# Rotary embedding of the queries: the sine product moved to VectorE and the exchange of halves moved to transfers

## The reference

```python
x = x + layernorm(attention(layernorm(x)))
x = x + layernorm(ffn(layernorm(x)))

# attention, per sequence
q = (x @ Wq.T).reshape(n, H, D);  kv = x @ Wkv.T;  kv_head = x @ Wkvh.T
kv_head = cumsum(kv_head * exp(cumsum(log_sigmoid(x @ Wg.T), shifted by one token)))
k = rope(outer(kp, kh));  v = outer(vp, vh)      # one key/value vector, one factor per head
o = softmax(causal(rope(q) @ k.T / sqrt(D))) @ v
return o @ Wout.T

# rope on a vector t with halves t1, t2
concat([t1 * cos - t2 * sin, t2 * cos + t1 * sin])
```

## Time and profile before

| | us |
|---|---|
| median of three runs | 1042.84 |
| lowest and highest run | 1042.63, 1044.16 |
| span of the profiled execution | 1040.7 |
| what lies around the span (median less span) | 2.1 |
| TensorE busy | 1025.2 |
| GpSimd busy | 936.1 |
| ScalarE busy | 870.2 |
| VectorE busy | 822.8 |

### The profile page before, as it was taken

One profiled execution on the slowest core, in us unless ns is written; L12 is line 12 of the kernel. 1 busy time (PEld: TensorE's weight loads), 2 busy tenths in 40 slices (PEclk: granted clock), 3 DMA queues, 4 the chain that ended last, 5 costly groups with the idle time before them and its releaser, 6 DMA issues.

```text
span 1040.7 us, 25126 instructions
## 1 busy us (share of the span) xinstructions
PE 1025.2 (99%) x7859; PEld 985.4 (95%) x7859; DVE 822.8 (79%) x2825; ACT 870.2 (84%) x2399; POOL 936.1 (90%) x926
## 2 busy tenths in 40 slices
PE   7999999999999999999999999999999999999997
PEld 6899999999999999999999999999999999999997
DVE  6868798878887888788788888887777656666665
ACT  5978898989898889898989898889888767777774
POOL 4889999999999999999999999999999758888875
PEclk9999999999999999999999999999999999999999
DMA  7561111112112111111121112111131000000001
GB/s 265 184 184 43 42 63 41 43 52 72 44 32 62 62 42 33 61 63 48 36 70 54 43 51 63 43 42 62 33 113 31 2 1 11 22 32 22 21 22 41
DMA packets 35124, 58.56 MB, mean 56 GB/s; under 512 B 3136, under 2 KB 16000, under 8 KB 34688
## 3 DMA queue, kind: packets, MB, share of 16 engines
q1 hardware_dynamic: 34992, 56.96, 16.9%
HBM read 50.92 MB, written 9.18 MB: 58 GB/s over the span
## 4 chain that ended last, share of the span: by engine, by line
POOL 59%; PE 20%; issue 15%; DVE 0%; POOLq 0%; ACT 0%; ACTq 0%; DVEq 0%
POOL arena L598 15%; POOL arena L621 14%; POOL arena L632 13%; POOL arena L608 12%; PE psum L1016 12%; PE psum L1057 6%; POOL arena L580 1%; POOL arena L556 1%; POOL X L589 1%; PE psum L774 1%; PE psum L1029 1%; PE psum L1038 1%; POOL arena L564 0%; POOLq L302 0%; POOL arena L571 0%
## 5 line engine op out<-in xcount | busy, mean ns | idle before, releaser
L632 POOL TENSOR_TENSOR arena<-arena 128x768 f32<-128x768 f32 x128 | 196.4, 1534 | 8.7 <-DVE arena L1580 8.3
L608 POOL TENSOR_TENSOR arena<-arena 128x512 f32<-128x512 f32 x128 | 174.4, 1363 | 10.0
L1593 DVE SCALAR_TENSOR_TENSOR pt_split<-psum,vh_col,pt_split 128x256 fp32r<-128x256 f32 (+1 forms) x512 | 177.0, 407 | 3.6 <-ACT pt_split L1252 3.0
L598 POOL TENSOR_TENSOR arena<-arena,tables 128x512 f32<-128x512 f32 x128 | 166.6, 1302 | 14.0 <-ACT arena L1222 13.2
L621 POOL TENSOR_TENSOR arena<-arena 128x512 f32<-128x512 f32 x127 | 163.1, 1284 | 0.0
L928 PE MATMUL psum<-arena 128*128 128x256 f32 x512 | 154.1, 383 | 3.1 <-POOL arena L608 1.8
L774 PE MATMUL psum<-wo_hi,o_hi 128*128 128x256 f32 x512 | 152.0, 297 | 0.0
L1233 ACT ACTIVATE arena<-arena 128x256 f32<-128x256 f32 x256 | 128.6, 502 | 26.6 <-DVE arena L1570 20.1
L774 PE MATMUL psum<-xt_lo,wq_hi 128*128 128x256 f32 x512 | 144.6, 282 | 0.0
L774 PE MATMUL psum<-xt_hi,wq_lo 128*128 128x256 f32 x512 | 144.4, 282 | 0.0
L774 PE MATMUL psum<-wo_hi,o_lo 128*128 128x256 f32 x512 | 144.2, 282 | 0.0
(11 more groups left out here) (194 smaller groups left out, 3411.7 us busy)
## 6 DMA issues: line engine op xcount, KB each, us to landing
arena<-kh_rows SPq DMA_DIRECT2D x127, 256.0 KB, 3.2
out<-spare SPq DMA_DIRECT2D x15, 256.0 KB, 2.2
arena<-w_rows SPq DMA_DIRECT2D x6, 512.0 KB, 4.7
X<-L_attn_Wout SPq DMA_DIRECT2D x1, 2048.0 KB, 14.3
X<-L_attn_x SPq DMA_DIRECT2D x1, 2048.0 KB, 12.7
arena<-L_attn_Wq SPq DMA_DIRECT2D x1, 1536.0 KB, 9.8
X<-L_attn_x SPq DMA_DIRECT2D x1, 1536.0 KB, 9.7
w_rows<-L_ffn_w_gate_up SPq DMA_DIRECT2D x3, 512.0 KB, 8.1
```

The source lines that it names most:

```text
L598: nc.gpsimd.tensor_tensor(swap, swap, spread, ALU.mult).then_inc(q_sined, 1)
L608: nc.gpsimd.tensor_tensor(q_rot[p % 2], q_cos[p % 2], q_swap[p % 2], ALU.add).then_inc(q_roped, 1)
L632: nc.gpsimd.tensor_tensor(tb, tb, r.unsqueeze(3).to_broadcast([P, HP, 3, P]), ALU.mult).then_inc(p_ready, 1)
L1593: last = nc.vector.scalar_tensor_tensor(pt_lo[p % 2][:, o], b[:, i], vh[:, t, h:h + 1], pt_hi[p % 2][:, o].bitcast(F32), ALU.mult, ALU.sub ...
```

## The change

The sine product is made before the halves are exchanged, by VectorE from `Q_BANK`, right behind the cosine product, into a new buffer `q_turned`. The halves of the product are then exchanged: for the first four pairs by ScalarE with two copies from SBUF, for the other 124 by two DMAs of 128 KB each on the sync engine's queue. GpSimd only adds. `q_swap` has one buffer in place of two. `Q_BANK` is free when the sine product is done (`q_sined`). The sine table changes its sign, since the product is now taken ahead of the exchange.

```diff
+SWAPS_ACT = 4
-        q_swap = [carve(HP, N) for _ in range(2)]
+        q_turned, q_swap = (carve(HP, N) for _ in range(2))
 # sync engine, called in each step behind spread_kh and the step's loads, ahead of next_load and store_chunk
+            def swap(g0, s):
+                at = pair_at(g0, s, LAG["swap"])
+                if at and at[0] >= SWAPS_ACT:
+                    g, half = at[0], D // 2
+                    sp.wait_ge(q_sined, g + 1)
+                    sp.wait_ge(q_roped, g)
+                    sp.dma_start(q_swap[0:half], q_turned[half:D]).then_inc(q_swapped, 16)
+                    sp.dma_start(q_swap[half:D], q_turned[0:half]).then_inc(q_swapped, 16)
 # GpSimd: queries_sin and its calls are gone
-                    pool.wait_ge(q_sined, g + 1)
                     pool.wait_ge(q_cosined, g + 1)
+                    pool.wait_ge(q_swapped, g * 32 + 32)
                     at_least(pool, s_ready, (g - 2) * HP + HP)
-                    nc.gpsimd.tensor_tensor(q_rot[p % 2], q_cos[p % 2], q_swap[p % 2], ALU.add).then_inc(q_roped, 1)
+                    nc.gpsimd.tensor_tensor(q_rot[p % 2], q_cos[p % 2], q_swap, ALU.add).then_inc(q_roped, 1)
 # TensorE: project, up, and the first step's keep_busy
-                    at_least(pe, q_swapped, g)
+                    at_least(pe, q_sined, g)
 # ScalarE: swap
-                if at:
-                    act.wait_ge(q_cosined, g + 1)
-                    at_least(act, q_roped, g - 1)
-                    nc.scalar.activation(flat[0:half, :], Q_BANK[half:D, :], ACT.Copy)
-                    nc.scalar.activation(flat[half:D, :], Q_BANK[0:half, :], ACT.Copy).then_inc(q_swapped, 1)
+                if at and at[0] < SWAPS_ACT:
+                    act.wait_ge(q_sined, g + 1)
+                    at_least(act, q_roped, g)
+                    nc.scalar.activation(q_swap[0:half], q_turned[half:D], ACT.Copy).then_inc(q_swapped, 16)
+                    nc.scalar.activation(q_swap[half:D], q_turned[0:half], ACT.Copy).then_inc(q_swapped, 16)
 # VectorE: queries_cos, behind the cosine product
+                    at_least(dve, q_swapped, g * 32)
+                    nc.vector.tensor_tensor(q_turned, heads(Q_BANK, N), sinq.unsqueeze(1).to_broadcast([P, HP, N]),
+                                            ALU.mult).then_inc(q_sined, 1)
 # table
-    return np.stack([c, s, c / np.sqrt(D), s / np.sqrt(D)], axis=1).astype(np.float32)
+    return np.stack([c, -s, c / np.sqrt(D), s / np.sqrt(D)], axis=1).astype(np.float32)
```

More of the change, by code:

```diff
@@ L499, in batch @@
                         sp.dma_start(X[:, half:TILES, :], tile_rows[:, half:TILES, :]).then_inc(x_rest, 16)
+                    swap(g0, s)
                     c0 = chunk_at(g0, s, "next_load")
@@ L589, in residual @@
                 nc.gpsimd.tensor_tensor(xs, xs, y_norm, ALU.add).then_inc(x1_done, PAIRS)
-            def queries_sin(g0, s):
-                at = pair_at(g0, s, LAG["rope"])
-                if at:
[L595 to L598, removed]
             def queries_add(g0, s):
@@ L728, in batch @@
                     if is_first(g0, s - 1) or is_first(g0, s - 2):
-                        queries_sin(g0, s + 1)
                         queries_add(g0, s + 1)
                     elif not is_first(g0, s - 3):
-                        queries_sin(g0, s)
                         queries_add(g0, s)
@@ L761, in _ @@
             key_rope(0, 0)
-            queries_sin(0, LAG["rope"])
             queries_add(0, LAG["rope"])
@@ L1002, in up @@
                 if u == 0 and c == 0:
-                    pe.wait_ge(q_swapped, STEPS)
+                    pe.wait_ge(q_sined, STEPS)
                     pe.wait_ge(s_max, STEPS * HP)
@@ L1113, in batch @@
                     if is_first(g0, s):
-                        pe.wait_ge(q_swapped, 1)
+                        pe.wait_ge(q_sined, 1)
                         keep_busy(Q_BANK, 3)
@@ L1214, in swap @@
                 at = pair_at(g0, s, LAG["swap"])
-                if at:
-                    g, p, _ = at
-                    half = D // 2
-                    act.wait_ge(q_cosined, g + 1)
-                    at_least(act, q_roped, g - 1)
-                    flat = q_swap[p % 2].rearrange("p h n -> p (h n)")
-                    nc.scalar.activation(flat[0:half, :], Q_BANK[half:D, :], ACT.Copy)
-                    nc.scalar.activation(flat[half:D, :], Q_BANK[0:half, :], ACT.Copy).then_inc(q_swapped, 1)
+                if at and at[0] < SWAPS_ACT:
+                    g, half = at[0], D // 2
+                    act.wait_ge(q_sined, g + 1)
+                    at_least(act, q_roped, g)
+                    nc.scalar.activation(q_swap[0:half], q_turned[half:D], ACT.Copy).then_inc(q_swapped, 16)
+                    nc.scalar.activation(q_swap[half:D], q_turned[0:half], ACT.Copy).then_inc(q_swapped, 16)
             def exponent(g0, s):
```

## The result

The changed kernel takes 1094.99 us (median of 4 runs, 1092.63 to 1097.26) against 1042.78 of the kernel before on the same chip (1042.63 to 1044.16). The ratio is 1.0497, with a 95% interval of 1.0479 to 1.0515: slower by 52 us. The forecast was 1069, slower by 26. The sign and the loop that it named are right; the size is half of what came, and the time lies outside the range. The profiled execution took 1094.13 us for a span of 1092.2.

The account below looks back on a forecast made before the run. TensorE was taken to bound the attention, with VectorE's loop as long as its step. 1040.7 + 20.3 (loop) + 6.5 (first batch) + 0.5 (last batch) - 1.5 (given back) = 1066.5 us span, median 1069, range 1053 to 1075.

Parts of the forecast that it names:

- the loop: VectorE's maxima, ScalarE's exponentials, reciprocal, cosine product, maxima again: no slack, added product 0.60 us per step, 20.3 us in all.
- the first batch: Pair 7's exchange queued behind the load of x, that load shifted by pair 6's exchange: 6.5 us late.
- L: Forecast loop length per step, cosine product to next cosine product: sum per batch 52.16 us with a weight chunk, 51.38 without.
- W: TensorE's step before the change, one pair's scores to the next's: 5.87 to 7.30 us, eight steps summing to 50.75.
- steps d to h stay: Of a batch's eight steps a to h, only a, b and c would lengthen, to 6.2 to 7.0 us from 5.9.
- so the term is nothing: Exchange transfers ahead of GpSimd's addition: scores no earlier than C + 5.38, inside split_pt's 5.46, so no added time.
- D: Time of the exchange transfers between sine product and addition: between 2.1 and 3.6 us, taken as 2.7.
- C: Start of a step's cosine product on VectorE; the next scores start at least 5.46 us after it, for split_pt.
- What is given back: TensorE's 3.7 us of waits for GpSimd's addition, mostly in the first batch: 1.5 us taken as won.
- Slow transfers: Rival: exchange transfers take D from 3.2 to 3.6 us, costing 27 to 42 us, total 1075 to 1091; chance 0.22.
- The idle VectorE: Rival: VectorE takes the product in its idle 8.6 us per batch, total 1042 to 1048; chance 0.09.
- the faster case: Rival: GpSimd's pace sets the steps, so relieving it by 1.30 us gives 1037 to 1040; chance 0.09.

Follow-up runs that it names:

- kernel 3: The changed kernel with ScalarE's copies exchanging the first 10 pairs in place of 4, transfers from pair 10 on: 1085.36 us, ratio 1.0408.
- kernel 4: The changed kernel with the cosine product left out, GpSimd adding the exchanged half to itself, transfers kept: 1051.29 us, ratio 1.009.
- kernel 9: The changed kernel with both exchange transfers issued from ScalarE's queue in place of the sync engine's: 1160.12 us, ratio 1.1121.
- the first two experiments: Kernel before plus an unread product behind each cosine product: 1109.84 us. Changed kernel with all exchanges by ScalarE's copies, no transfers: 1085.27 us.
- kernel 7: The changed kernel with sine product first, cosine product behind the maxima, all exchanges by ScalarE's copies, no transfers: 1043.97 us, ratio 1.0012.
- kernel 10: The kernel before with an extra product, both inputs in SBUF, on VectorE behind the maxima: 1085.95 us, ratio 1.0418.
- kernels 8 and 9: Both transfers issued by ScalarE: 8 with cosine product behind the maxima and copies for 10 pairs, 1074.42 us; 9 in the changed kernel, 1160.12 us.
- kernel 1: The kernel before with one extra unread product, both inputs in SBUF, on VectorE behind each cosine product: 1109.84 us, ratio 1.0638.

## Why the prediction was right in sign and half in size

**Where the missing time lies.** The span was forecast at 1066.5 us and is 1092.2. Of the 25.7 us between them, 10.0 are late exchanges, which the sum had at nothing; 7.5 are the loop, which was mis-sized; 5.7 the first batch (10.7 for 5.0), 1.9 the last (3.4 for 1.5), and 0.4 what lies behind the last scores.

**The loop: right in mechanism, too small in size.** The cosine products of the batch shown stand 6.22, 6.48, 7.06, 6.21, 6.55, 6.23, 6.65 and 7.10 us apart; the forecast L was 6.16, 6.42, 7.01, 6.17, 6.63, 6.17, 6.95 and 6.65. Step b after, VectorE:

```profile
364.60 0.68 DVE L1553 TENSOR_TENSOR arena<-psum,tables 128x512 f32<-128x512 f32 x1
...
369.73 0.20 DVE L1581 RECIPROCAL arena<-arena 128x8 f32<-128x8 f32 x1 [0.56 <-ACT arena L1233]
...
371.08 0.68 DVE L1553 TENSOR_TENSOR arena<-psum,tables 128x512 f32<-128x512 f32 x1
```

From the cosine product to the reciprocal it is 5.13 us (forecast 5.08), and 1.35 on to the next product (1.34). In the six batches of 50.9 us the loss is the forecast 1.4. In the other eight it is 2.3. The forecast for these 14 was 19.3 us (20.3 with the last batch's 1.0), and 26.8 came. 2.1 of the 7.5 between them lie in W: I took 50.75 us from one batch for all, and before the change the batches are 50.60 in the mean (step f is 6.39 us in one kind and 6.05 in the other). The other 5.4 are loops that are longer than the 52.16 at which I had them settle. In an undisturbed batch of the first kind (from pair 55's cosine product) they add up to 52.50 us, in one of the second kind (from pair 79's) to 52.64: nearly the same, whatever TensorE's own batch is. Step h's 7.10 for my estimate of 6.65 is the largest single miss. The second kind loses more because its own length before was only 50.4 us; I had taken one length for both kinds. My sign that steps d to h stay didn't fit my own recurrence either, by which d grows to 7.01; it is 7.05.

**The transfers, "so the term is nothing": the step that failed.** I took D = 2.7 and a gate of C + 5.38, inside the 5.46 of split_pt. An undisturbed exchange in the trace after, rows of VectorE, the sync engine, GpSimd and TensorE's loader in order of time:

```profile
310.81 0.68 DVE L1556 TENSOR_TENSOR arena<-psum,tables 128x512 f32<-128x512 f32 x1
311.51 0.46 SPq L486 DMA_DIRECT2D arena<-arena  x1
312.02 0.60 SPq L487 DMA_DIRECT2D arena<-arena  x1
314.54 1.29 POOL L611 TENSOR_TENSOR arena<-arena 128x512 f32<-128x512 f32 x1 [1.60 <-issue]
315.88 0.30 PEld L928 LDWEIGHTS psum<-arena 128*128 128x128 f32 x2 [0.22 <-POOL arena L611]
```

Issue to landing is 2.86 us in the median, and the second DMA is issued 0.51 behind the first. The gate is C + 5.6 and so above split_pt's. By itself these 0.15 us are small, since the loop sets the pace anyway. What I had not priced is that a gate without slack passes on every late arrival: I had one value for D, and no late exchanges at all. The same rows of a late one:

```profile
324.57 0.67 DVE L1556 TENSOR_TENSOR arena<-psum,tables 128x512 f32<-128x512 f32 x1
325.27 0.46 SPq L486 DMA_DIRECT2D arena<-arena  x1
325.78 0.59 SPq L487 DMA_DIRECT2D arena<-arena  x1
329.95 1.27 POOL L611 TENSOR_TENSOR arena<-arena 128x512 f32<-128x512 f32 x1 [3.71 <-issue]
331.27 0.70 PE L928 MATMUL psum<-arena 128*128 128x256 f32 x2 [1.65 <-POOL arena L611]
```

It was issued as promptly (0.70 us behind the start of the sine product) and landed 4.56 us after its first issue, 1.7 us later than usual. In this stretch the DMA view shows a packet of the queue that loads instructions, and in the undisturbed one it doesn't:

```profile
q1 hardware_dynamic: 192, 0.28, 27.6%
q8 instruction: 1, 0.02, 1.8%
```

Its kinds are the transfers of the kernel (q1) and the loading of instructions (q8). (A 16 KB store of factors, issued 1.1 us behind the exchange, also lies in this stretch; but every batch has such a store behind the same pair, and no other exchange there is late.) There are eight late exchanges (over 3.6 us) among pairs 11 to 127, one in each of the seven disturbed batches and one in the last: 10.0 us and part of the last batch's 3.4. Five of them (32, 45, 68, 94, 112) overlap such a packet. Of the exchanges that overlap one between 1 us behind their first issue and their landing, 5 of 17 are late; of the others, 3 of 100. (Counted from the issue itself it is 5 of 24 and 3 of 93.) In kernel 3 it is 3 of 16 and 2 of 101, but in kernel 4 it is 2 of 20 and 10 of 97. That is an association and no proof; no run here took these packets away. For 22 and 102 the order of the queue is plain: the sync engine stood at L473 until a store of factors, itself issued behind a chunk's load, had landed (36.7 us in 15 places, above); then it issued a 256 KB row and, 0.4 us behind it, the exchange, 1.0 and 0.9 us late, which took 4.5 and 4.4 us more. 120 is issued promptly, while three of the six chunks of the last batch and a row behind them are still under way, and takes 4.2 us: as forecast in kind, 1.3 us late where I had 0.5.

**The first batch: half.** The load of x ahead of pair 7's exchange costs what the prediction said, and in the way it said: the load lands at 74.6 and the exchange at 75.2, 0.7 behind (I had 1). But the load is issued at 60.28 and not at 56.61, and takes 14.3 us and not 12.7: 5.3 us together, and the scores forecast for 71.7 start at 76.7. The later issue is not the exchanges' doing. In kernel 3, which has none on the sync engine there, that engine's timeline has

```profile
59.58 0.59 SPq L510 DMA_DIRECT2D X<-L_attn_x  x1
```

so 3.0 of the 3.7 us come from the loop (with ScalarE's copies in it, in that kernel), which lengthens the first eight steps as well (pair 7's scores at 68.5 in kernel 3 for 66.0 before, 2.5 us). I had let the loop's loss begin at pair 7. The rest, 8.2 us, is the transfers', forecast at 6.5. The sync engine's rows in the full change:

```profile
57.12 0.53 SPq L506 DMA_DIRECT2D w_rows<-L_ffn_w_proj  x1
57.75 0.54 SPq L486 DMA_DIRECT2D arena<-arena  x1
...
59.60 0.64 SPq L509 DMA_DIRECT2D arena<-L_ffn_w_gate_up  x1
60.28 0.65 SPq L510 DMA_DIRECT2D X<-L_attn_x  x1
67.04 0.53 SPq L486 DMA_DIRECT2D arena<-arena  x1
```

and GpSimd's additions of pairs 6 and 7:

```profile
65.70 1.27 POOL L611 TENSOR_TENSOR arena<-arena 128x512 f32<-128x512 f32 x1 [7.34 <-issue]
...
75.36 1.27 POOL L611 TENSOR_TENSOR arena<-arena 128x512 f32<-128x512 f32 x1 [5.73 <-issue]
```

Pair 6's exchange, behind the 512 KB copy within DRAM (57.12) and a 256 KB row (56.74), landed 7.8 us after its issue; I had counted 0.8 for it. In kernel 9 it was issued at 57.67, 1.9 us ahead of that copy, and the addition followed at 60.65. Whether the copy holds it up by the queue's order or by the traffic isn't separated by these runs. For pair 7 both play a part: behind the load in one queue it waits for the load's end, on another it still takes 8.0 us.

**What is given back** (1.5 us): nothing that could be seen. Waits of 3.7 us were there to win; the first batch, where most of them lay, became the place of the largest new ones.

**The rivals.** Slow transfers, 1075 to 1091, was nearest in time but not in mechanism: D is 2.9, below its 3.2. I had also mis-worked its price: put into the recurrence, D = 3.2 (a gate of C + 5.88) gives 52.17 us per batch and D = 3.6 gives 53.34, so 1.4 and 2.6 us more and not 1.8 and 2.8. At D = 3.2 the rival is hardly apart from the forecast. The idle VectorE and the faster case fell with the first two experiments. No version here beats the kernel before; the best of them, 7, is 0.12% slower.

## What to carry to other kernels

An engine's idle time belongs to a place in its order. Before work is moved onto an engine that looks free, follow the loop through it and the engines that it releases and waits for; an instruction behind the one that releases the others, and ahead of the one that waits for them, can be nearly free (kernel 7: 1.3 us in all), and the same instruction inside a loop without slack is paid in every step (41 us here). It is free only if it disturbs no other engine there: kernel 10's product, in the same place but with both inputs in SBUF, cost 43 us. If a transfer replaces a computed step on the path to the bounding engine, count the slack behind its landing and not only its median, and look at what else is loaded in that moment, on any queue. In these kernels the one queue delayed a few exchanges, and the second queue many more.

## What the runs showed of the hardware

- Two DMAs of 128 KB within SBUF, the halves of the partitions exchanged, issued 0.51 us apart by the sync engine, land 2.86 us after the first issue in the median. Issued by ScalarE instead, while the sync engine's rows ran free, 48 of 117 land over 3.6 us behind the sine product, against 8. In kernels 8 and 9 a 256 KB row issued from 2 us ahead to 1 us behind the first issue went with a median of 4.57 and 4.72 us (2.89 without).
- A 128x512 product on VectorE takes 0.67 to 0.69 us with one input in PSUM, and 0.67 to 1.98 us (mean 0.995, kernel 1) with both in SBUF beside a busy GpSimd, whose product of the same size goes from 1.28 to 1.69 us; in kernel 10 it is 1.13 us in the mean, and GpSimd's addition goes from 1.36 to 1.53 us. The Trainium skill (GPSIMD Engine Reference, "Specifications") names this: GpSimd's SBUF interfaces are shared with VectorE, and they contend when VectorE has two inputs in SBUF. The rows of kernels 1 and 10 agree and give the size.
- The granted clock went to 1.2 GHz for 3.4 us in 14 places of kernel 9, behind standstills of TensorE of 1.8 to 3.1 us; matmuls then start 0.21 us apart in place of 0.12. Seven others of 1.7 to 2.4 us there, and those of 2.07 and 1.65 us before pairs 22 and 45 of the full change, had none behind them.
